# Attention on one core: corrections of the maxima as powers of e on GpSimd, and a quarter of a head's outputs copied by VectorE, three quarters by ScalarE

## The chip, the cores and the metric

The kernel runs on one core of a Trainium2 chip. The metric is the device time of one execution in microseconds (us); of several runs the median counts.

## The reference

One transformer block on `x` of 2 sequences, 2048 tokens, 256 features, all in float32. Six modulation vectors come from a small conditioning input. Then:

```python
h = _layernorm(x) * (1 + ca) + sa
q, k, v = h @ query_proj, h @ key_proj, h @ value_proj     # 16 heads; key size 16, value size 64
attn = softmax(q k^T / 4, axis=1)                          # over the QUERY positions, for each key
o = attn @ v                                               # for each query, a sum over the keys
x = x + ga * (o @ output_proj)
h = _layernorm(x) * (1 + cb) + sb
x = x + gb * down(silu(gate(h)) * up(h))                   # 704 hidden; weights and inputs quantised to FP4 in blocks of 16
```

The softmax runs over the query positions. So a key on a partition has all the 2048 scores that belong to one softmax along its row, and the normalising factor can be multiplied into the value row of that key.

## The kernel before

**Phases.** For each of the 2 sequences (`b`) there is a short preparation (normalised tokens, queries, keys, values) and then attention; at the end one pass over 32 token tiles does the output projection and the feed-forward part. Attention fills most of the time: its first maximum starts at 78.5 us for sequence 0 and at 750.8 us for sequence 1, and its last product starts at 1372.5 us.

**Attention.** Loop variable `j` runs over 256 tiles of 128 keys (16 heads, 16 tiles in each; `i` is the tile within its head). Each tile has two halves of 1024 queries; a half is called a unit here, `u = 2j + half`. For a unit:

- TensorE (`scores`) writes 128 keys by 1024 queries into one of three PSUM slots, `slot[u % 3]`, in 4 matmuls on quarters of the array. It first waits until ScalarE has read the unit three before (`exped`).
- VectorE (`maximum`, line 1070) reduces the slot to the negated maximum `nm` of each key.
- ScalarE (`exponent`, line 812) writes exp(score - maximum) to a ring of 8 tiles in SBUF, `e_sb`, with the row sums in `ssum`.

The two halves of a row have different maxima. For each group of 4 tiles (`g`) the two are reconciled: GpSimd computes the differences `dlt` (lines 1305 to 1309) after tile 4g+3's maxima; ScalarE computes `cor = exp(dlt)` (line 840) in tile 4g+4, after that tile's first exponent; GpSimd then computes the total, its reciprocal as a power of -1 (line 1282), the factors, and the scaled values `vp` for both halves (line 1296).

**Sum over keys.** TensorE (`attend`, line 603) multiplies `vp` by `e_sb` seven tiles later (`jv = j - LAG`, `LAG = 7`) and accumulates a whole head in `acc`, two PSUM banks, 1024 columns. TensorE's order in one `j` is: scores of half 0, half of tile jv's products (8 matmuls), scores of half 1, the other half. On a head's first tile (`begins`) both scores come first and then all 16 matmuls of the tile.

**End of a head.** After the last products of a head, in j with i = 6, VectorE copies `acc[:, 0:512]` to SBUF (`ost`, line 1083), after both of its maxima of that j; ScalarE copies `acc[:, 512:1024]` (line 834) between its two exponents of that j. `took_low` and `took_high` count these. The first products of the next head overwrite `acc` and wait for both counts. GpSimd later splits `ost` in two parts (`split_head`, in tiles with i = 9, 10, 13, 14) and SyncE's queue stores them.

**Order.** Each engine runs the list that the code writes, in that order, with counting semaphores between engines; there is no planner. SyncE only issues DMAs. At the end of sequence 0 GpSimd also computes `rstd` of the next sequence's tokens (`inverse_root`) behind the last `vp`, and TensorE's turning of those tokens (`turn_tokens`, line 457) stands within the last tiles' products.

Of the kernel before, what the change touches and what calls it, by code (L numbers as in the profile page):

```python
# [9 lines left out]
ALU = mybir.AluOpType  # L10
ACT = mybir.ActivationFunctionType
AX = mybir.AxisListType

B, N, D, H, VD, F = 2, 2048, 256, 16, 64, 704
HV = H * VD
P = 128
# [6 lines left out]
SQUARE = (2.0 ** 23 / 12.0) ** 0.5  # L23
FLOOR = 5461.0 * 1024.0
LEAST = 1e-30
GROUP = 4
NG = NT // GROUP
JT = H * NT
JG = JT // GROUP
UNITS = 2 * JT  # L30
# [55 lines left out]
def adaln_block(nc, x, cT, wmod, wq, wk, wv, wo, wgu, wd, out):  # L86
    ctx = ExitStack()
    with ctx:
        def sb(name, shape, dt=F32):
            return ctx.enter_context(nc.sbuf_tensor(name, shape, dt))  # L90
# [4 lines left out]
        def tally(name, step=1):  # L95
            return Tally(ctx.enter_context(nc.semaphore(name)), step)
# [4 lines left out]
        pe, act, dve, pool, sp = nc.tensor, nc.scalar, nc.vector, nc.gpsimd, nc.sync  # L101
# [31 lines left out]
        ost = place("ost", [P, 1024], OST_AT)  # L133
# [3 lines left out]
        ssum = sb("ssum", [P, 4, GROUP, 2])  # L137
        dlt = sb("dlt", [P, 4, GROUP, 2])
# [2 lines left out]
        tot = sb("tot", [P, 4, GROUP])  # L141
        rtot = sb("rtot", [P, 4, GROUP])
        mone = sb("mone", [P, GROUP])
        fac = sb("fac", [P, 4, GROUP, 2])
        st6 = sb("st6", [P, NG, GROUP, 6])
        mv = sb("mv", [P, NG, GROUP, 2])
# [112 lines left out]
        out_out = [tally(f"out_out{s}", 16) for s in range(3)]  # L259

        made_ident, made_half, rstd_made, wv_low = tally("made_ident"), tally("made_half"), tally("rstd_made"), tally("wv_low")
        diff_made, vp_made = tally("diff_made"), tally("vp_made")
        wsq_made, root_made = tally("wsq_made"), tally("root_made")
        wo_split, wd_folded, spread = tally("wo_split"), tally("wd_folded"), tally("spread")
        head_split = tally("head_split")
# [2 lines left out]

        c_exp, wqk_high, wv_high, tok_out = tally("c_exp"), tally("wqk_high"), tally("wv_high"), tally("tok_out")
        part_high, v_act, gu_turned = tally("part_high"), tally("v_act"), tally("gu_turned")  # L270
        dn_turned, exped, cor_made, took_high = tally("dn_turned"), tally("exped"), tally("cor_made"), tally("took_high")
        wgu_high, wdb_high, xq_high, hq_high = tally("wgu_high"), tally("wdb_high"), tally("xq_high"), tally("hq_high")
        silu_made, mix_squared, zx_made = tally("silu_made"), tally("mix_squared"), tally("zx_made")

# [186 lines left out]
        def take_quarter(b, kind, n):  # L461

            q, before = uses[b][kind, n]
            if before:
                pe.wait_ge(*quarter_read(before))
            elif b == 0 and q < 2:
                pe.wait_ge(*mod_cols.past(0))
            elif b and q < 2:
                pe.wait_ge(*exped.past(b * UNITS - 1))
            elif b:  # L470
                pe.wait_ge(*(took_low if q == 2 else took_high).past(b * H - 1))
            return quarter[q]

        def bounds():
# [136 lines left out]
        def project(i):  # L611
            u, r = divmod(i, 2)
            b = i // NT
            if r == 0:
                pe.wait_ge(*o_in[u % 2].past(u // 2))
            if i % NT == 0:
                pe.wait_ge(*wo_split.past(8 * b + 7))
            if i < 3:
                pe.wait_ge(*exped.past(B * UNITS - 1))
            elif i == 3:  # L620
                pe.wait_ge(*took_low.past(B * H - 1))
            else:
                pe.wait_ge(*x2_made.past(i - 1))
            products(proj[i], [(o_r[:, u % 2, 1, c, r * P:(r + 1) * P], o_r[:, u % 2, 0, c, r * P:(r + 1) * P],
                                wo_lo[b][:, c, :], wo_hi[b][:, c, :]) for c in range(8)]).then_inc(proj_mm.sem)
# [189 lines left out]
        def attend_act(b):  # L815
            act.wait_ge(*v_mm.past(2 * (b * NT + EARLY) - 1))
            for p in range(2):
                for r in range(4):
                    act.wait_ge(*part_out[p][r].past(b * NG // 2 + 1))
            for j in range(JT + LAG):  # L820
                jv = j - LAG
                if j == ERING - 2:
                    act.wait_ge(*v_mm.past(2 * (b * NT + 3 * GROUP) - 1))
                if j == ERING - 1:
                    act.wait_ge(*v_mm.past(2 * (b * NT + NT) - 1))
                if b + 1 < B and j in (JT + 4, JT + 6):
                    take_tokens(b + 1, (j - JT) // 2 - 2)
                for half in range(2):
                    if half == 1 and jv >= 0 and jv % NT == NT - 1:
                        h = jv // NT  # L830
                        act.wait_ge(*attended.past(b * JT + jv))
                        if b * H + h >= 1:
                            act.wait_ge(*o_out.past(b * H + h - 1))
                        act.copy(ost[:, 512:1024], acc[:, 512:1024]).then_inc(took_high.sem)
                    if j < JT:
                        exponent(b, j, half)
                    if half == 0 and j % GROUP == 0 and GROUP <= j <= JT:
                        g = j // GROUP - 1
                        act.wait_ge(*diff_made.past(b * JG + g))
                        act.activation(cor[:, g % 4], dlt[:, g % 4], ACT.Exp).then_inc(cor_made.sem)  # L840
                if j < NT - EARLY:
                    take_values_act(b, EARLY + j)
                if j == JT + 2 and b == B - 1:
                    act.wait_ge(*vp_made.past(B * JG - 1))
                    for k in range(2):
                        high(wgu_hi[k][:, :], wguT[:, k, :]).then_inc(wgu_high.sem)
                    stretch(0)
                    square(1)
                    stretch(1)
# [222 lines left out]
        def attend_dve(b):  # L1072
            for j in range(JT + LAG):
                jv = j - LAG
                for half in range(2):
                    if j < JT:
                        maximum(b, j, half)
                if jv >= 0 and jv % NT == NT - 1:
                    h = jv // NT
                    dve.wait_ge(*attended.past(b * JT + jv))  # L1080
                    if b * H + h >= 1:
                        dve.wait_ge(*o_out.past(b * H + h - 1))
                    dve.tensor_copy(ost[:, 0:512], acc[:, 0:512]).then_inc(took_low.sem)  # L1083
                if j < NT - EARLY:
                    take_values_dve(b, EARLY + j)
                if j == JT + 2 and b + 1 < B:
                    stats(b + 1, 0)
                    stats(b + 1, 1)
                    normalise(b + 1, 0)
                    normalise(b + 1, 1)  # L1090
                    stats(b + 1, 2)
                    low_tokens(b + 1, 0)
                    stats(b + 1, 3)
                    normalise(b + 1, 2)
                if j == JT + 6 and b + 1 < B:
                    low_tokens(b + 1, 1)
                    normalise(b + 1, 3)
                if j == JT + 2 and b == B - 1:
                    dve.wait_ge(*wgu_high.past(1))
                    dve.wait_ge(*attended.past(B * JT - 5))  # L1100
                    dve.wait_ge(*got_rows.past(0))
                    for i in range(2):
                        token_moments(i)
                        low(dve, wgu_lo[:, i, :], wguT[:, i, :], wgu_hi[i][:, :]).then_inc(wgu_low.sem)
                    mix_normalise(1)
                    mix_snap(1)
# [162 lines left out]
        def attend_pool(b):  # L1269
            for j in range(JT + LAG):  # L1270
                g = j // GROUP - 1
                s = g % 4
                if j % GROUP == 0 and GROUP <= j <= JT:
                    pool.wait_ge(*cor_made.past(b * JG + g))
                    sem, n = pool_own.next()
                    pool.tensor_tensor(wsum[:, s], cor[:, s], ssum[:, s], ALU.mult).then_inc(sem)  # L1276
# [23 lines left out]
                if j % GROUP == GROUP - 1 and j < JT:  # L1300
                    g, s = j // GROUP, j // GROUP % 4
                    pool.wait_ge(*maxed.past(b * UNITS + 2 * j + 1))
                    if g >= 4:
                        pool.wait_ge(*cor_made.past(b * JG + g - 4))
                    pool.tensor_tensor(dlt[:, s, :, 0], nm[:, s, :, 1], nm[:, s, :, 0], ALU.subtract)  # L1305
                    sem, n = pool_own.next()
                    pool.tensor_tensor(dlt[:, s, :, 1], nm[:, s, :, 0], nm[:, s, :, 1], ALU.subtract).then_inc(sem)
                    pool.wait_ge(sem, n)
                    pool.tensor_scalar(dlt[:, s], dlt[:, s], 0.0, None, ALU.min).then_inc(diff_made.sem)
                if j == JT + 2 and b + 1 < B:  # L1310
                    for g in range(NG):
                        inverse_root(b + 1, g)
# [55 lines left out]
        def gpsimd_program():  # L1368
# [3 lines left out]
                               pattern=[[-1, P]], channel_multiplier=1).then_inc(made_ident.sem)  # L1372
            pool.memset(quarter4[:, :, :], -0.25)
            pool.memset(mone[:, :], -1.0)
            pool.memset(epsilon, EPS)
            pool.memset(zero, 0.0)
            pool.memset(wdT[:, FCH - 1, :], 0.0)
# [56 lines left out]
```

## Time and profile before

| | |
|---|---|
| median of 3 runs | 1696.1 us (1695.29 to 1697.58) |
| profiled execution, its own time | 1700.96 us |
| its span, first to last instruction | 1699.6 us |
| granted TensorE clock, mean | 0.994 of full |
| TensorE matmul busy | 1646.5 us (97%) |
| VectorE busy | 1591.2 us (94%) |
| ScalarE busy | 1364.8 us (80%) |
| GpSimd busy | 779.4 us (46%) |
| moved by DMA | 123.15 MB, mean 72 GB/s |

Busy time is the union of an engine's instructions from first start to last end. Matmuls are pipelined and their ends are modelled, so 97% doesn't mean that TensorE is at its peak. A VectorE or ScalarE instruction's duration includes filling and draining; the next one may start before it ends. "Idle before" is the time in which an engine did nothing before instructions of a group, with the instruction that ended it.

### The profile page before, as it was taken

The numbers are of one execution on the slowest core, as the hardware profiler recorded it, in microseconds if no ns is written. First come the engines' busy times: TensorE is split into PE (matmuls) and PEld (weight loads), VectorE is DVE, ScalarE is ACT, GpSimd is POOL, SyncE is SP. The second block draws the span as 40 slices with busy tenths as digits, with TensorE's granted clock in tenths as the row PEclk, the third lists the DMA queues.
The fourth block names the chain that finished last, engine by engine and source line by source line (L and its number), as shares of the span: only waits on it lengthen the run. The fifth ranks groups of instructions, "written<-read, shape, count | busy, mean of one in ns | idle before, by whom it ended". The sixth has DMA issues, their size and how long they took to land.

```text
span 1699.6 us, 38849 instructions
## 1 busy us (share of the span) xinstructions
PE 1646.5 (97%) x15446; PEld 818.5 (48%) x15446; DVE 1591.2 (94%) x1726; ACT 1364.8 (80%) x2490; POOL 779.4 (46%) x1625
## 2 busy tenths in 40 slices
PE   9999999999999999999999999999999999999998
PEld 8743333333332333664333333333333379999997
DVE  6989999999999999769999999999999869988887
ACT  5389999999999999638999999999999933333332
POOL 3024444544444445303544454566645447644552
PEclk8999999999999999999999999999999999999999
DMA  6202111111111112411111112111111544434420
GB/s 223 72 2 70 51 51 49 45 45 56 61 51 51 47 45 75 156 48 35 46 52 47 45 45 67 53 51 51 46 45 45 154 133 125 149 125 148 153 67 19
DMA packets 83103, 123.15 MB, mean 72 GB/s; under 512 B 4706, under 2 KB 69098, under 8 KB 82922
## 3 DMA queue, kind: packets, MB, share of 16 engines
q1 hardware_dynamic: 82506, 120.15, 22.3%
q8 instruction: 121, 1.98, 0.5%
q14 instruction: 60, 0.49, 0.1%
q10 hardware_dynamic: 416, 0.53, 0.1%
HBM read 74.52 MB, written 46.15 MB: 71 GB/s over the span
## 4 chain that ended last, share of the span: by engine, by line
DVE 65%; PE 29%; ACT 2%; issue 2%; POOL 1%; DMA 1%; SPq 0%; ACTq 0%; POOLq 0%; DVEq 0%
DVE nm L1070 60%; PE acc L436 11%; PE slot L436 9%; PE acc L603 5%; ACT e_sb L812 2%; PE slot L659 1%; DVE ost L1083 1%; PE slot L574 1%; DVE v_sb L1030 1%; DMA v_sb<-in_wmod 0%; PE acc L634 0%; PE slot L457 0%; DVE qs L1137 0%; DMA qk_parts<-e_sb 0%; DVE e_sb L1125 0%
## 5 line engine op out<-in xcount | busy, mean ns | idle before, releaser
L1070 DVE TENSOR_REDUCE nm<-slot 128x1 f32<-128x1024 f32 x1024 | 1166.1, 1213 | 8.1 <-PE slot L574 5.9
L812 ACT ACTIVATE e_sb<-slot,nm 128x1024 f32<-128x1024 f32 x1024 | 1137.3, 1113 | 23.9 <-DVE nm L1070 19.0
L603 PE MATMUL acc<-e_sb,vp 64*64 64x512 f32 x8192 | 1060.7, 594 | 6.7 <-DVE ost L1083 4.7
L574 PE MATMUL slot<-stq,stk 64*64 64x512 f16 x4096 | 412.0, 388 | 21.6 <-ACT e_sb L812 21.6
L574 PEld LDWEIGHTS slot<-stq,stk 64*64 64x64 f16 x4096 | 117.7, 103 | 626.7 <-ACT e_sb L812 589.5
L603 PEld LDWEIGHTS acc<-e_sb,vp 64*64 64x64 f32 x8192 | 283.4, 132 | 188.4 <-issue 74.2
L1305 POOL TENSOR_TENSOR dlt<-nm 128x4 f32<-128x4 f32 x128 | 25.9, 202 | 422.7 <-DVE nm L1070 422.7
L812 ACT ACTIVATION_READ_ACCUMULATOR e_sb<-slot,nm 128x1 f32 x1024 | 199.6, 195 | 0.0
L1296 POOL TENSOR_TENSOR vp<-v_sb,fac 128x512 f32<-128x512 f32 x128 | 133.6, 1044 | 10.2 <-POOL fac L1286 0.3
L1282 POOL TENSOR_TENSOR rtot<-tot,mone 128x4 f32<-128x4 f32 x128 | 132.8, 1038 | 10.0
L1276 POOL TENSOR_TENSOR wsum<-cor,ssum 128x8 f32<-128x8 f32 x128 | 26.0, 203 | 233.4 <-ACT cor L840 233.4
L916 POOL TENSOR_TENSOR ost<-ost,ost_hi 128x256 fp32r<-128x256 f32 x128 | 93.6, 731 | 10.3
L731 ACT CAST xqT_hi<-acc 128x256 fp32r<-128x256 f32 x32 | 11.9, 373 | 106.7 <-PE acc L634 106.6
L436 PE MATMUL slot<-wgu_hi,xqT_hi 128*128 128x352 f32 x256 | 83.6, 327 | 7.1 <-DVE xqT_lo L916 7.1
L885 ACT ACTIVATE e_sb<-slot 128x704 f32<-128x704 f32 x32 | 24.3, 760 | 78.3 <-PE slot L436 78.3
L436 PE MATMUL slot<-wgu_lo,xqT_hi 128*128 128x352 f32 x256 | 82.6, 323 | 0.0
L436 PE MATMUL slot<-wgu_hi,xqT_lo 128*128 128x352 f32 x256 | 82.6, 322 | 0.0
L1362 POOL TENSOR_TENSOR e_sb<-e_sb,qs 128x256 f32<-128x256 f32 x32 | 21.4, 669 | 113.8 <-DVE e_sb L1153 113.8
L1247 POOL CAST ost_hi<-ost 128x256 fp32r<-128x256 f32 x128 | 55.7, 435 | 0.7 <-DVE ost L1083 0.7
L436 PE MATMUL acc<-wdb_hi,hqT_lo 128*128 128x256 f32 x192 | 54.2, 282 | 0.0
L436 PE MATMUL acc<-wdb_hi,upper 128*128 128x256 f32 x192 | 54.0, 281 | 0.0
L436 PE MATMUL acc<-wdb_lo,upper 128*128 128x256 f32 x192 | 54.0, 281 | 0.0
(180 smaller groups left out, 1940.3 us busy)
## 6 DMA issues: line engine op xcount, KB each, us to landing
o_r<-o_heads SPq DMA_DIRECT2D x32, 1024.0 KB, 7.4
stk<-qk_parts SPq DMA_DIRECT2D x128, 128.0 KB
o_heads<-ost_hi SPq DMA_DIRECT2D x64, 256.0 KB, 3.4
o_heads<-ost SPq DMA_DIRECT2D x64, 256.0 KB, 4.1
v_sb<-in_x SPq DMA_DIRECT2D x16, 512.0 KB, 6.6
qk_parts<-e_sb SPq DMA_DIRECT2D x32, 256.0 KB, 2.9
stq<-qk_parts SPq DMA_DIRECT2D x128, 64.0 KB
out<-e_sb SPq DMA_DIRECT2D x32, 128.0 KB, 1.8
```

The source lines that it names most:

```text
L436: mm = pe.matmul(o, a, w, start=(n == 0 and m == 0), stop=(n == len(pairs) - 1 and m == 2))
L574: mm = pe.matmul(slot[s][side * VD:(side + 1) * VD, c * 512:(c + 1) * 512], stk[c * 64:c * 64 + 64, h % 2, i * P + side * VD:i * P + (side ...
L603: mm = pe.matmul(acc[half * VD:(half + 1) * VD, c * 512:(c + 1) * 512], vp[rows, g % 3, gi, half, :], e_v[rows, j % ERING, n0:n0 + 512], s ...
L812: act.activation(e_v[:, j % ERING, half * 1024:(half + 1) * 1024], slot[u % 3][:, :], ACT.Exp, bias=nm[:, g % 4, i, half:half + 1], accum_ ...
L885: act.activation(sg[:, i % 2, :].rearrange("p (a b) -> p a b", b=352), gu[0][:, :].rearrange("p (a b) -> p a b", b=512)[:, :, 0:352], ACT. ...
L916: return eng.tensor_tensor(dst, full, hi.bitcast(F32), ALU.subtract)
L1070: dve.tensor_reduce(nm[:, g % 4, i, half:half + 1], slot[u % 3][:, :], AX.X, ALU.max, negate=True).then_inc(maxed.sem)
L1247: pool.tensor_copy(ost_hi[:, part], ost[:, part]).then_inc(sem)
L1276: pool.tensor_tensor(wsum[:, s], cor[:, s], ssum[:, s], ALU.mult).then_inc(sem)
L1282: pool.tensor_tensor(rtot[:, s, :], tot[:, s, :], mone[:, :], ALU.pow).then_inc(sem)
L1296: pool.tensor_tensor(vp[:, g % 3], v_v[:, i0:i0 + GROUP, h * VD:(h + 1) * VD].unsqueeze(2).to_broadcast([P, GROUP, 2, VD]), fac[:, s].unsq ...
L1305: pool.tensor_tensor(dlt[:, s, :, 0], nm[:, s, :, 1], nm[:, s, :, 0], ALU.subtract)
```

## The change

Three things change.

- The correction `cor` is computed by GpSimd as a power with base e, 8 elements per partition, right after `dlt`. `dlt` is also bounded below at -87.3. ScalarE no longer computes `cor`. GpSimd's sum now waits for `exped` of the first exponent of tile 4g+4 (for the row sums), which before was implied by the wait for ScalarE's `cor`. For a sequence's last group there is no such exponent; there ScalarE copies two sums to a scratch tile after its last exponent and counts `summed`.
- VectorE copies columns 0 to 255 of `acc`, ScalarE columns 512 to 1023 as before and then columns 256 to 511, in a second copy that waits for VectorE's copy (`took_low`). `took_high` is counted by ScalarE's second copy.
- Two waits of TensorE on `took_low` outside the head loop (`take_quarter`, `project`) become waits on `took_high`.

```diff
@@ scalar: attend_act, end of a head and corrections
-                        act.copy(ost[:, 512:1024], acc[:, 512:1024]).then_inc(took_high.sem)
+                        act.copy(ost[:, 512:1024], acc[:, 512:1024])
+                        act.wait_ge(*took_low.past(b * H + h))
+                        act.copy(ost[:, 256:512], acc[:, 256:512]).then_inc(took_high.sem)
                     if j < JT:
                         exponent(b, j, half)
-                    if half == 0 and j % GROUP == 0 and GROUP <= j <= JT:
-                        g = j // GROUP - 1
-                        act.wait_ge(*diff_made.past(b * JG + g))
-                        act.activation(cor[:, g % 4], dlt[:, g % 4], ACT.Exp).then_inc(cor_made.sem)
+                if j == JT:
+                    act.wait_ge(*exped.past((b + 1) * UNITS - 1))
+                    act.copy(sums_last[:, :], ssum[:, (JG - 1) % 4, GROUP - 1, :]).then_inc(summed.sem)
@@ vector: attend_dve
-                    dve.tensor_copy(ost[:, 0:512], acc[:, 0:512]).then_inc(took_low.sem)
+                    dve.tensor_copy(ost[:, 0:256], acc[:, 0:256]).then_inc(took_low.sem)
@@ gpsimd: attend_pool
                 if j % GROUP == 0 and GROUP <= j <= JT:
+                    if j < JT:
+                        pool.wait_ge(*exped.past(b * UNITS + 2 * j))
+                    else:
+                        pool.wait_ge(*summed.past(b))
                     pool.wait_ge(*cor_made.past(b * JG + g))
...
                     pool.wait_ge(*maxed.past(b * UNITS + 2 * j + 1))
-                    if g >= 4:
-                        pool.wait_ge(*cor_made.past(b * JG + g - 4))
...
-                    pool.tensor_scalar(dlt[:, s], dlt[:, s], 0.0, None, ALU.min).then_inc(diff_made.sem)
+                    pool.tensor_scalar(dlt[:, s], dlt[:, s], 0.0, LEAST_EXP, ALU.min, ALU.max).then_inc(diff_made.sem)
+                    pool.wait_ge(*diff_made.past(b * JG + g))
+                    pool.tensor_tensor(cor[:, s], euler[:, :, :], dlt[:, s], ALU.pow).then_inc(cor_made.sem)
@@ tensor: take_quarter and project
-                pe.wait_ge(*(took_low if q == 2 else took_high).past(b * H - 1))
+                pe.wait_ge(*took_high.past(b * H - 1))
...
-                pe.wait_ge(*took_low.past(B * H - 1))
+                pe.wait_ge(*took_high.past(B * H - 1))
```

## Rows read from the trace of the kernel before

**Rows 1.** The page's busy time: engine, us, share, instructions.
```profile
PE 1646.5 (97%) x15446; PEld 818.5 (48%) x15446; DVE 1591.2 (94%) x1726; ACT 1364.8 (80%) x2490; POOL 779.4 (46%) x1625
```

**Rows 2.** Chain of waits, one head of sequence 0: start us, us, what.
```profile
216.67 0.61 DVE ost L1083
...
217.40 1.95 PE acc L603 x16
...
219.60 32.48 DVE nm L1070 x29
...
256.60 1.22 DVE nm L1070
```

**Rows 3.** Timeline at a head's end: start, us, engine, line, operation, count, idle before.
```profile
216.59 0.68 DVE L1083 COPY ost<-acc 128x512 f32<-128x512 f32 x1
216.68 0.58 ACT L834 COPY ost<-acc 128x512 f32<-128x512 f32 x1
...
217.15 1.13 ACT L812 ACTIVATE e_sb<-slot,nm 128x1024 f32<-128x1024 f32 x1
...
217.40 1.95 PE L603 MATMUL acc<-e_sb,vp 64*64 64x512 f32 x16 [0.16 <-DVE ost L1083]
...
219.14 0.42 PE L574 MATMUL slot<-stq,stk 64*64 64x512 f16 x4
...
219.60 3.52 DVE L1070 TENSOR_REDUCE nm<-slot 128x1 f32<-128x1024 f32 x3
```

**Rows 4.** Groups by shape, VectorE and ScalarE: busy us, mean ns, idle.
```profile
L1070 DVE TENSOR_REDUCE nm<-slot 128x1 f32<-128x1024 f32 x1024 | 1166.1, 1213 | 8.1 <-PE slot L574 5.9
...
L1083 DVE COPY ost<-acc 128x512 f32<-128x512 f32 x32 | 21.7, 678 | 0.0
...
L834 ACT COPY ost<-acc 128x512 f32<-128x512 f32 x32 | 18.5, 577 | 0.3 <-PE acc L603 0.3
...
L1170 DVE TENSOR_TENSOR e_sb<-e_sb,acc 128x256 f32<-128x256 f32 x32 | 13.1, 409 | 2.1 <-PE acc L436 2.1
...
L731 ACT CAST xqT_hi<-acc 128x256 fp32r<-128x256 f32 x32 | 11.9, 373 | 106.7 <-PE acc L634 106.6
```

**Rows 5.** Groups by shape: the powers that GpSimd computes.
```profile
L1282 POOL TENSOR_TENSOR rtot<-tot,mone 128x4 f32<-128x4 f32 x128 | 132.8, 1038 | 10.0
...
L1342 POOL TENSOR_TENSOR rstd<-ve,mhalf 128x1 f32<-128x1 f32 x32 | 18.2, 569 | 0.0
```

**Rows 6.** Timeline of one group of four key tiles in mid-head.
```profile
199.62 17.05 DVE L1070 TENSOR_REDUCE nm<-slot 128x1 f32<-128x1024 f32 x15
...
201.36 0.24 POOL L1309 TENSOR_SCALAR dlt<-dlt 128x8 f32<-128x8 f32 x1
...
202.00 1.11 ACT L812 ACTIVATE e_sb<-slot,nm 128x1024 f32<-128x1024 f32 x1
...
203.39 0.20 POOL L1276 TENSOR_TENSOR wsum<-cor,ssum 128x8 f32<-128x8 f32 x1 [1.79 <-ACT cor L840]
...
203.67 0.20 POOL L1279 TENSOR_TENSOR tot<-wsum 128x4 f32<-128x4 f32 x1
...
205.34 1.04 POOL L1296 TENSOR_TENSOR vp<-v_sb,fac 128x512 f32<-128x512 f32 x1
...
206.65 0.41 PE L574 MATMUL slot<-stq,stk 64*64 64x512 f16 x4
...
206.89 1.03 PE L603 MATMUL acc<-e_sb,vp 64*64 64x512 f32 x8
```

**Rows 7.** Timeline at the end of sequence 0.
```profile
682.30 0.24 POOL L1309 TENSOR_SCALAR dlt<-dlt 128x8 f32<-128x8 f32 x1
...
683.20 0.20 POOL L1276 TENSOR_TENSOR wsum<-cor,ssum 128x8 f32<-128x8 f32 x1 [0.65 <-ACT cor L840]
...
688.63 1.09 PE L457 MATMUL slot<-ident,e_sb 128*128 128x128 f32 x8 [0.17 <-DVE e_sb L939]
```

**Rows 8.** Chain of waits after sequence 0's last head.
```profile
697.17 0.49 ACT ost L834
```

More of the change, by code:

```diff
@@ L25 @@
 LEAST = 1e-30
+EULER = 2.718281828459045
+LEAST_EXP = -87.33654
 GROUP = 4
@@ L143, in adaln_block @@
         mone = sb("mone", [P, GROUP])
+        euler = sb("euler", [P, GROUP, 2])
+        sums_last = sb("sums_last", [P, 2])
         fac = sb("fac", [P, 4, GROUP, 2])
@@ L261, in adaln_block @@
         made_ident, made_half, rstd_made, wv_low = tally("made_ident"), tally("made_half"), tally("rstd_made"), tally("wv_low")
-        diff_made, vp_made = tally("diff_made"), tally("vp_made")
+        diff_made, vp_made, cor_made = tally("diff_made"), tally("vp_made"), tally("cor_made")
         wsq_made, root_made = tally("wsq_made"), tally("root_made")
@@ L270, in adaln_block @@
         part_high, v_act, gu_turned = tally("part_high"), tally("v_act"), tally("gu_turned")
-        dn_turned, exped, cor_made, took_high = tally("dn_turned"), tally("exped"), tally("cor_made"), tally("took_high")
+        dn_turned, exped, summed, took_high = tally("dn_turned"), tally("exped"), tally("summed"), tally("took_high")
         wgu_high, wdb_high, xq_high, hq_high = tally("wgu_high"), tally("wdb_high"), tally("xq_high"), tally("hq_high")
@@ L1374, in gpsimd_program @@
             pool.memset(mone[:, :], -1.0)
+            pool.memset(euler[:, :, :], EULER)
             pool.memset(epsilon, EPS)
```

## The prediction

> **What bounds the kernel now.** I read the page's busy times first, then the chain of waits, then the timeline at the place where the chain changes engines. TensorE, VectorE and ScalarE are all close to full [rows 1], so the busy shares alone don't say who sets the pace. The chain does: in each head VectorE's maxima stand for 32.48 us, and the next head starts 256.60 - 219.60 = 37.00 us later [rows 2]. The reader is to see what lies in the other 4.5 us: one more maximum, VectorE's copy of the outputs, TensorE's 16 products, one set of scores, and back to the maxima.
>
> In mid-head VectorE alone is the bound: 15 maxima in 17.05 us [rows 6] with 1.21 us for one [rows 4] are (17.05 - 1.21) / 14 = 1.131 us from start to start. 32 of them are 36.19 us. The copy takes 0.68 us and the maxima overlap by 0.08, so it costs 0.60: 36.79 us. The period is 37.00. The missing 0.2 us is idle time of VectorE, and the timeline shows where [rows 3]: the copy starts at 216.59, so the third maximum after it could start at 216.59 + 0.60 + 2 x 1.13 = 219.45, but starts at 219.60. Its scores started only at 219.14, behind the 16 products that started at 217.40. And those waited for the copies, which ended at 216.59 + 0.68 = 217.27 (VectorE) and 216.68 + 0.58 = 217.26 (ScalarE). So at a head's end VectorE is already ahead of TensorE. What starts the next head is the later of two copies, which today end together.
>
> **The change, part by part.**
>
> *VectorE's copy, 512 to 256 columns.* From 678 ns for 512 columns and 1213 for 1024 the slope is 1.04 ns per column, so 256 columns take 678 - 267 = 411 ns; VectorE's 256-column operation out of the same tensor takes 409 [rows 4]. VectorE's own work per head falls by 0.27 us. The copy would end at 217.00.
>
> *ScalarE's second copy.* It can issue 217.15 - 216.68 = 0.47 us after the first, the distance at which the next instruction now starts [rows 3]. VectorE's copy is over by then (217.00), so the added wait costs nothing. Its duration: the nearest row is ScalarE's 256-column cast out of the same tensor, 373 ns; by the slope from this copy to the 1024-column exponent (1114 - 577 over 512 columns) it would be 308 [rows 3, 4]. I take 373. It ends at 217.15 + 0.37 = 217.52, where the later copy now ends at 217.27: the release of TensorE is 0.25 us later. Lower end: 308 ns, 0.18 us later. Upper end: the second copy waits until the first is drained (0.58 + 0.37), 0.36 us later. A gain is excluded: the second copy can't start before the first is issued, and its end would have to lie before 217.27.
>
> *Who waits.* Queued behind the second copy on ScalarE is the second exponent of that tile: it starts 0.26 us later (the second copy's distance, 0.47 less 0.21 for 256 columns) and ends near 218.54 instead of 218.28; the scores behind the 16 products need it at 219.14 and later, so that is covered. TensorE is not covered: in order, it has nothing to do before the 16 products. They and the following scores move by 0.25. VectorE, now ready at 216.59 + 0.33 + 2.26 = 219.18, waits until 219.60 + 0.25 = 219.85. Its idle time there grows from 0.15 to 0.67 us. VectorE's shorter copy isn't returned, since VectorE was ahead at this point already; the head's period becomes 37.25 us. TensorE's later pace doesn't repair it: what comes after are 29 maxima at VectorE's own pace.
>
> This happens at 15 ends of heads in each sequence: 30 x 0.25 = 7.5 us.
>
> A rule against the split: the Trainium skill (ScalarE: Activation LUTs, What ACT_TABLE_LOAD costs) gives 186 ns plus 0.833 ns per column for an instruction with immediate operands, with about 93 ns of overlap, and Advanced Engine Details and Errata (The Read-Write Bubble) advises large tiles for that reason. By this estimate the copies of 512 and 256 end 0.61 - 0.09 + 0.40 = 0.92 us after the start, 217.60, and 30 ends of heads would cost 9.9 us instead of 7.5. The trace has the 512-column copy at 577 ns, under the page's 613, so I keep the rows.
>
> *Corrections on GpSimd.* ScalarE loses 128 exponents of 8 columns. A gain would need VectorE to wait for what ScalarE releases, and in mid-head it starts a maximum every 1.131 us, right behind the one before [rows 6]: 0. GpSimd gains 128 powers of 8 elements. Rows: 1038 ns for 4 elements, 569 for 1 [rows 5], so 156 ns per element and 1038 + 4 x 156 = 1.66 us. Ends: 1.04 (no dependence on size), 2.08 (twice the row of 4). In mid-head `dlt` is ready at 201.36 + 0.24 = 201.60 and the sum starts at 203.39 [rows 6]. With 0.08 us between dependent steps (203.39 + 0.20 to 203.67) the power is done at 201.60 + 0.08 + 1.66 = 203.34, and the sum starts at 203.42; the exponent that it must also wait for ends at 203.11. So `vp` moves by 0.03 us. It ends now at 206.38, and TensorE takes it at 206.89: some 0.4 us to spare. With 2.08 us `vp` comes 0.45 later: at the edge. Behind it stands a second reserve: TensorE's scores end at 207.06, and VectorE's next start after that is 199.62 + 7 x 1.131 = 207.54. So a power costs nothing until about 1.63 + 0.4 + 0.45 = 2.5 us. The same cover holds for the two-operation `dlt`. In four heads of sequence 1 GpSimd also folds the output weights and its queue is fullest; I count on the same reserve there: 0, or some tenths of a microsecond in all. Its splitting of `ost` starts two tiles after the copies and isn't reached by 0.25 us.
>
> *End of sequence 0.* Here no later exponent stands in between: the sum starts at 683.20, 0.66 us after `dlt` at 682.54. With the power it starts at 682.54 + 0.08 + 1.66 + 0.08 = 684.36, 1.15 us later, and `vp` and the next tokens' `rstd` with it. TensorE has already waited for them, 0.17 us at 688.63 [rows 7], so all 1.15 goes through. ScalarE's last copy is on the chain there as well, at 697.17, and GpSimd's splitting waits for it [rows 8]: 0.25 more. Together 1.4 us. (Ends: 0.54 + 0.18 = 0.7 and 1.57 + 0.36 = 1.9.) At the end of sequence 1 TensorE has the first projections between; I take 0.
>
> **Sum.** 7.5 + 1.4 = 8.9 us, from 0.18 x 30 + 0.7 = 6.1 to 0.36 x 30 + 1.9 = 12.7. The profiled execution's own time is 1700.96 us, so it would be 1709.9. The median shown is 1696.1, 0.3% lower; on it the forecast is 1705.0 (+0.5%).
>
> **Rivals.**
>
> *VectorE's saving counts.* The chain names VectorE's copy at every head's end and its maxima for the rest [rows 2]; a bound engine that sheds 0.27 us should give it back: 30 x 0.27 = 8 us, 1688.0. This needs TensorE to start the products no later than now, and to make up time in the first units of a head. Against it: ScalarE's half already ends with VectorE's (217.26 and 217.27), it can't finish 256 more columns in no time, and VectorE idles right after [rows 3]. Faster.
>
> *Nothing moves.* The 0.13 us between the copies' end and the first product is TensorE's own time and swallows part of the delay, the second copy is shorter than its lower end, and the end of sequence 0 has more slack than the 0.17 us wait says: within 3.4 us, 1696 to 1699.
>
> *GpSimd's chain binds.* If the power of 8 elements with varying exponents takes over 2.5 us, `vp` is late in every group that isn't at the start of a head: with 3.0 us about 0.5 us in some 100 groups, 50 us, near 1755. For it: rows show only the fixed exponents -1 and -0.5. Against it: those two, and 1 and 4 elements, lie on a plausible line that ends far below 2.5.
>
> **How the numbers follow.** The forecast has 0.72, VectorE's saving 0.09, nothing 0.12, GpSimd 0.07. What a measurement of this kernel can tell from no change is about 0.2%, 3.4 us. So faster 0.09, same 0.12, slower 0.79. The forecast's own range is 1702 to 1709. Eight in ten: from 1696, which takes in the upper part of no change, to 1711, which takes in the sum's upper end and a little of GpSimd's case.
>
> **What would show it.** Right: the chain at a head's end goes over ScalarE's copy, not VectorE's; two copies on ScalarE of about 577 and 373 ns, the 16 products starting some 0.9 to 1.0 us after the first (now 0.72); a period of 37.25 us; VectorE's idle time after the copy near 0.7 us; the power at 1.66 us; TensorE's wait at the turn of the sequences near 1.3 us. Wrong: a period at or below 37.00; `vp` on the chain in mid-head; a second copy that starts before 0.47 us or waits for VectorE; a total outside 1702 to 1709.

## The result, and the profile after

The changed kernel took 1703.73 us (median of 5 runs, 1703.44 to 1705.22), the kernel before beside it 1697.58 us (5 runs, 1695.29 to 1698.56): ratio 1.0039, 95% interval 1.0028 to 1.0051, or +6.6 us by the ratio (the medians themselves lie 6.2 us apart). A second comparison of the same two kernels (below, after_again) gave 1.0052, 1.0040 to 1.0065, or +8.8 us by the ratio (medians 10.2 us apart). It is slower, as forecast, by about the size forecast (1705.0 us, range 1696 to 1711).

The profiled execution of the changed kernel took 1703.73 us itself, with a span of 1702.4 us and a mean granted clock of 1.000. The one of before took 1700.96 us at 0.994. Here only 2.8 us lie between them, and a large part of what follows is about that.

The page's busy time after the change (columns as in [rows 1]):

```profile
PE 1639.4 (96%) x15446; PEld 812.3 (48%) x15446; DVE 1582.1 (93%) x1726; ACT 1368.7 (80%) x2396; POOL 977.6 (57%) x1754
```

VectorE sheds 9.1 us against [rows 1], GpSimd gains 198 us, ScalarE 4, although it runs 94 instructions fewer: the small exponents had stood almost wholly within the records of their neighbours (0.2 us of the busy time was theirs alone), while the second copies have 5.2 us to themselves. So the slower kernel has less work on the engine that was its bound in mid-head. The busy shares can't say why.

The chain of waits over one head of sequence 0 (start us, us, what), against [rows 2]:

```profile
213.91 0.39 ACT ost L841
...
214.44 1.95 PE acc L608 x16
...
216.65 1.24 DVE nm L1077
...
251.18 0.39 ACT ost L841
...
253.92 1.24 DVE nm L1077
```

Two things are to be seen. In front of TensorE's 16 products stands ScalarE's second copy, where VectorE's copy stood. And the period, the time from one head to the next, is 253.92 - 216.65 = 37.27 us where it was 37.00 [rows 2]. Between the ends of heads the chain now follows ScalarE's exponents instead of VectorE's maxima; the two run in step there.

The timeline at a head's end (columns as in [rows 3]):

```profile
213.36 0.41 DVE L1090 COPY ost<-acc 128x256 f32<-128x256 f32 x1
213.45 0.57 ACT L839 COPY ost<-acc 128x512 f32<-128x512 f32 x1
...
213.91 0.38 ACT L841 COPY ost<-acc 128x256 f32<-128x256 f32 x1
...
214.44 1.95 PE L608 MATMUL acc<-e_sb,vp 64*64 64x512 f32 x16 [0.43 <-ACT ost L841]
...
216.65 5.79 DVE L1077 TENSOR_REDUCE nm<-slot 128x1 f32<-128x1024 f32 x5 [0.61 <-PE slot L579]
```

VectorE is done at 213.77, ScalarE's second copy at 214.29. The products start 0.99 us after ScalarE's first copy, where it was 217.40 - 216.68 = 0.72 [rows 3]. All of the 0.27 reaches the maxima: the wait of VectorE for the scores is now a row of its own, 0.61 us. Over all heads the same is seen in the waits (engine and line, for whom, total us, times, longest); the line of before, then that of after:

```profile
PE acc L603 <- DVE ost L1083: 4.7, 30, 0.2
```

```profile
PE acc L608 <- ACT ost L841: 12.9, 30, 0.4
```

30 waits grew by 8.2 us in all. The groups by shape (busy us, mean ns, idle) give the prices that [rows 4, 5] had to bound:

```profile
L1321 POOL TENSOR_TENSOR cor<-euler,dlt 128x8 f32<-128x8 f32 x128 | 210.8, 1647 | 10.6
...
L1319 POOL TENSOR_SCALAR dlt<-dlt 128x8 f32<-128x8 f32 x128 | 24.7, 193 | 11.2
...
L839 ACT COPY ost<-acc 128x512 f32<-128x512 f32 x32 | 18.4, 576 | 0.3 <-PE acc L608 0.3
...
L1090 DVE COPY ost<-acc 128x256 f32<-128x256 f32 x32 | 13.1, 410 | 0.0
...
L841 ACT COPY ost<-acc 128x256 f32<-128x256 f32 x32 | 12.3, 383 | 0.0
```

At the end of sequence 0 (timeline; against [rows 7]) the power stands alone between `dlt` and the sum:

```profile
682.63 0.19 POOL L1319 TENSOR_SCALAR dlt<-dlt 128x8 f32<-128x8 f32 x1
...
682.91 1.65 POOL L1321 TENSOR_TENSOR cor<-euler,dlt 128x8 f32<-128x8 f32 x1
...
684.70 0.20 POOL L1288 TENSOR_TENSOR wsum<-cor,ssum 128x8 f32<-128x8 f32 x1
...
687.72 1.95 PE L608 MATMUL acc<-e_sb,vp 64*64 64x512 f32 x16 [0.64 <-POOL vp L1308]
...
690.10 1.09 PE L462 MATMUL slot<-ident,e_sb 128*128 128x128 f32 x8 [0.44 <-DVE e_sb L946]
```

The sum starts 2.07 us after `dlt`, where it was 683.20 - 682.30 = 0.90 [rows 7]. TensorE waits 0.64 + 0.44 = 1.08 us instead of 0.17. From the start of the sequence's last maximum to TensorE's turning (L462; L457 before) it is 9.20 us, and was 8.06: 1.14 us more. This distance is called "the turn" below.

**The account of the two profiled executions.** 30 x 0.273 us (the period is 37.269 in both sequences, 36.996 before) is 8.2 us; the end of sequence 0 brings 1.14: 9.3 us. Seen were 2.8. Both traces can be cut at the starts of the same instructions (the 17th maximum of a sequence, because its first few differ in time where the clock fell just ahead of them):

| stretch | before, us | after, us | difference |
|---|---|---|---|
| up to the first maximum | 78.49 | 74.81 | -3.68 |
| to the 17th maximum | 30.16 | 30.07 | -0.09 |
| to the last maximum of sequence 0 | 571.91 | 576.02 | +4.11 |
| to ScalarE's last copy of the values (L767; L772 after) | 63.58 | 64.58 | +1.00 |
| to the 17th maximum of sequence 1 | 37.29 | 35.86 | -1.43 |
| to the last maximum of sequence 1 | 571.91 | 576.00 | +4.09 |
| to the end | 346.29 | 345.07 | -1.22 |

The third and the sixth row are the heads, 15 x 0.273 = 4.10 each, as it should be. The fourth is the 1.14 of the turn, but for 0.14. The other rows became shorter. The stretches at three of these places, of before and then of after (from:to, length, busy time of each engine, granted clock, DMA share, GB/s):

```profile
0.00:20.00 20.00, 17.55 (x89) 17.12 (x90) 10.68 (x42) 6.46 (x10) 4.18 (x15) 0.70 0.83 288
745.00:755.00 10.00, 7.42 (x43) 4.63 (x41) 5.03 (x6) 4.58 (x11) 0.00 (x0) 0.83 0.14 51
1390.00:1400.00 10.00, 7.81 (x49) 7.29 (x48) 8.07 (x11) 3.25 (x5) 6.10 (x8) 0.83 0.01 2
```

```profile
0.00:20.00 20.00, 17.62 (x112) 16.58 (x113) 12.56 (x51) 8.18 (x13) 4.21 (x16) 1.00 0.83 290
745.00:755.00 10.00, 7.41 (x48) 4.87 (x47) 6.48 (x8) 4.66 (x12) 0.00 (x0) 1.00 0.14 50
1390.00:1400.00 10.00, 6.41 (x43) 5.68 (x42) 9.72 (x14) 2.71 (x5) 5.13 (x7) 1.00 0.27 85
```

The number before the last two is the granted clock, the share of TensorE's full speed. The profiled execution of before ran parts of all three places at TensorE's lower level (1.2 GHz), that of after none. By the table the changed kernel gained 3.68 + 0.09 us at the first place, 1.43 at the second and 1.22 at the third, 6.4 in all: 9.3 - 6.4 - 0.1 = 2.8, as was seen. So the next question was whether the change has anything to do with the clock.

### The profile page after: what moved, and what is told of

Read it like the earlier page. It is cut to its first block, busy times and chain, and to the rows that moved or that the text cites. A ratio compares the mean times of both kernels' runs of the same rounds, so it can differ in the third digit from the quotient of the medians.

```text
span 1702.4 us, 38892 instructions
## 1 busy us (share of the span) xinstructions
PE 1639.4 (96%) x15446; PEld 812.3 (48%) x15446; DVE 1582.1 (93%) x1726; ACT 1368.7 (80%) x2396; POOL 977.6 (57%) x1754
## 4 chain that ended last, share of the span: by engine, by line
ACT 41%; PE 28%; issue 22%; DVE 8%; POOL 1%; DMA 0%; SPq 0%; POOLq 0%; ACTq 0%; DVEq 0%
ACT e_sb L817 39%; PE acc L441 10%; PE slot L441 9%; PE acc L608 5%; DVE nm L1077 4%; PE slot L664 1%; ACT ost L841 1%; PE slot L579 1%; DVE v_sb L1037 1%; ACT ost L839 0%; PE acc L447 0%; PE acc L639 0%; DVE qs L1144 0%; DMA qk_parts<-e_sb 0%; PE slot L462 0%
## 5 line engine op out<-in xcount | busy, mean ns | idle before, releaser
L1321 POOL TENSOR_TENSOR cor<-euler,dlt 128x8 f32<-128x8 f32 x128 | 210.8, 1647 | 10.6
L1308 POOL TENSOR_TENSOR vp<-v_sb,fac 128x512 f32<-128x512 f32 x128 | 133.4, 1042 | 10.2 <-POOL fac L1298 0.3
L1294 POOL TENSOR_TENSOR rtot<-tot,mone 128x4 f32<-128x4 f32 x128 | 129.2, 1009 | 10.0
```

The lines of the kernel that those rows point to most:

```text
L1294: pool.tensor_tensor(rtot[:, s, :], tot[:, s, :], mone[:, :], ALU.pow).then_inc(sem)
L1308: pool.tensor_tensor(vp[:, g % 3], v_v[:, i0:i0 + GROUP, h * VD:(h + 1) * VD].unsqueeze(2).to_broadcast([P, GROUP, 2, VD]), fac[:, s].unsq ...
L1321: pool.tensor_tensor(cor[:, s], euler[:, :, :], dlt[:, s], ALU.pow).then_inc(cor_made.sem)
```

## Experiments

The theory: TensorE's release at each head's end is set by the later of two copies; the change makes ScalarE's later by 0.27 us; the power costs something only at the end of sequence 0; the clock of the three places varies from run to run in either kernel. The rivals: the powers cost time in mid-head too; VectorE's shorter copy gives something back; the change itself raised the clock. Each kernel was timed beside the kernel before.

**before_again: the kernel before, unchanged.**

> The kernel before, unchanged, for a second trace. In the first trace TensorE's granted clock was 0.70 of full from 0 to 20 us and lower again near 749 and 1395 us; the changed kernel's trace has 1.00 throughout. If these drops belong to an execution, this trace may lack them, and then its own time is near 1694.5 us (1700.96 less some 6.5 us that the three places cost), with the head's period at 37.00 us. If they belong to the kernel's program, they are there again at the same three places. Times: within 0.2% of the kernel before.

1697.58 us (11 runs), ratio 1.0004 (0.9995 to 1.0013); its profiled execution took 1698.29 us at a mean clock of 0.997. The same three stretches:

```profile
0.00:20.00 20.00, 17.65 (x109) 16.44 (x110) 11.74 (x46) 7.32 (x12) 4.17 (x15) 0.91 0.83 292
745.00:755.00 10.00, 9.62 (x51) 6.70 (x52) 5.64 (x6) 5.71 (x13) 0.00 (x0) 0.83 0.14 50
1390.00:1400.00 10.00, 8.80 (x54) 8.56 (x55) 7.98 (x12) 3.37 (x5) 4.28 (x8) 0.83 0.01 2
```

Neither alternative of the expectation came out whole: the places recur, but the amount differs (0.91 at the start, where it was 0.70), and the first maximum starts at 75.66 us instead of 78.49, which is what the profiled execution was faster by. The places aren't fixed for every variant: in less_vector (below) the last stretch at the lower level begins at 1525 us instead of near 1395, and power_twice has four, near 776, 1209, 1462 and 1595 us, and none in the first 20.

**split_only: the copies alone, added to the kernel before, with the two waits outside the head loop; the corrections stay on ScalarE.**

```
-  act.copy(ost[:, 512:1024], acc[:, 512:1024]).then_inc(took_high.sem)
+  act.copy(ost[:, 512:1024], acc[:, 512:1024])
+  act.wait_ge(*took_low.past(b * H + h))
+  act.copy(ost[:, 256:512], acc[:, 256:512]).then_inc(took_high.sem)
-  dve.tensor_copy(ost[:, 0:512], acc[:, 0:512]).then_inc(took_low.sem)
+  dve.tensor_copy(ost[:, 0:256], acc[:, 0:256]).then_inc(took_low.sem)
```

> Only the copies changed (VectorE 256 columns, ScalarE 512 and 256), the corrections stay on ScalarE. Release theory (the head's period is set by the later copy): period 37.27 us as in the changed kernel, 30 x 0.27 = 8.1 us over the kernel before, and TensorE's wait at the turn of the sequences unchanged at 0.17 us. VectorE theory (its saving counts): period 36.73, 8 us less.

1706.29 us (5 runs), ratio 1.0053 (1.0039 to 1.0067), period 37.269 us, the turn 8.06 us as before. Its timeline at a head's end:

```profile
215.57 0.57 ACT L834 COPY ost<-acc 128x512 f32<-128x512 f32 x1
...
216.04 0.38 ACT L836 COPY ost<-acc 128x256 f32<-128x256 f32 x1
...
216.56 1.95 PE L603 MATMUL acc<-e_sb,vp 64*64 64x512 f32 x16 [0.43 <-ACT ost L836]
```

The same 0.99 us, the same wait of 0.43. The whole cost per head is the copies'. Three of its runs had a mean clock of 0.996 (1706.1 to 1706.7 us), like 15 runs of the kernel before (median 1698.3): 8.0 us, where 30 x 0.273 is 8.2.

**powers_only: the changed kernel with the copies as before** (and the two waits outside the head loop).

```
-  dve.tensor_copy(ost[:, 0:256], acc[:, 0:256]).then_inc(took_low.sem)
+  dve.tensor_copy(ost[:, 0:512], acc[:, 0:512]).then_inc(took_low.sem)
-  act.copy(ost[:, 512:1024], acc[:, 512:1024])
-  act.wait_ge(*took_low.past(b * H + h))
-  act.copy(ost[:, 256:512], acc[:, 256:512]).then_inc(took_high.sem)
+  act.copy(ost[:, 512:1024], acc[:, 512:1024]).then_inc(took_high.sem)
```

> Only the corrections moved to GpSimd, the copies as before (512 and 512). Release theory: period 37.00 us, nothing in mid-head; the sum after the last group of sequence 0 comes 1.15 us later, so about +1.1 us in all, within what can be told from no change. A rival in which ScalarE's freed 25 us count: faster by up to 0.1 us per group, 12 us. A rival in which GpSimd's longer chain delays the scaled values in every group: slower by 0.1 us or more per group, 12 us or more.

1697.12 us (11 runs), ratio 1.0004 (0.9995 to 1.0013); period 36.996 us, the turn 9.20. 128 powers of 1.65 us cost nothing in mid-head, and 1.14 us at the turn. The interval of the medians holds that 1.14 us (ratio 1.0007) and 0. Runs at the same clock show it: at 0.999 they took 1696.9 and 1697.1 us and those of the kernel before 1695.9 (median of 17), at 0.998 1698.4 and 1697.3 (median of 19), at 1.000 1695.6 to 1696.2 and 1694.4 (one run); only at 0.997 there is no difference (1697.6 and 1698.2 against 1698.3).

**last_on_scalar: the changed kernel, but the last group of each sequence has its correction from ScalarE's exponent.**

```
-  act.wait_ge(*exped.past((b + 1) * UNITS - 1))
-  act.copy(sums_last[:, :], ssum[:, (JG - 1) % 4, GROUP - 1, :]).then_inc(summed.sem)
+  act.wait_ge(*diff_made.past(b * JG + JG - 1))
+  act.activation(cor[:, (JG - 1) % 4], dlt[:, (JG - 1) % 4], ACT.Exp).then_inc(summed.sem)
...
-  pool.wait_ge(*cor_made.past(b * JG + g))
+  if j < JT:
+      pool.wait_ge(*cor_made.past(b * (JG - 1) + g))
...
+  if g < JG - 1:
...
       pool.tensor_tensor(cor[:, s], euler[:, :, :], dlt[:, s], ALU.pow).then_inc(cor_made.sem)
```

> The changed kernel, but each sequence's last group has its correction computed by ScalarE again. If the power behind the last group is the second term of the sum, TensorE's wait for the next sequence's tokens falls from some 1.3 us to near 0.2 us and the last products of sequence 0 end 1.1 us earlier; the period stays 37.27. Total: 1.1 us under the changed kernel, +8 us against the kernel before. If this term is given back later (in the preparation of sequence 1), the total doesn't move.

1704.72 us (5 runs), ratio 1.0048 (1.0033 to 1.0062); period 37.269 us, the turn 8.04. The timeline there:

```profile
684.42 0.19 POOL L1320 TENSOR_SCALAR dlt<-dlt 128x8 f32<-128x8 f32 x1
...
685.03 0.20 ACT L847 ACTIVATE cor<-dlt 128x8 f32<-128x8 f32 x1
685.32 0.20 POOL L1289 TENSOR_TENSOR wsum<-cor,ssum 128x8 f32<-128x8 f32 x1 [0.71 <-ACT cor L847]
```

The sum is back at 0.90 us after `dlt`, and the 1.16 us of the turn are gone. The median doesn't show it: the one run at a mean clock of 1.000 took 1702.0, and those of the changed kernel at this clock 1703.4 to 1704.0; but its one run at 0.996 took 1708.0, and the changed kernel's at this clock 1707.8 and 1708.0. These are few runs. The trace shows the turn; that the total falls with it isn't shown by this kernel.

**less_vector, less_both, less_scalar: the kernel before with one or both copies at half width from the second head on.** The columns that are then copied by nobody are left out of the output.

```
less_vector, less_both:
-  dve.tensor_copy(ost[:, 0:512], acc[:, 0:512]).then_inc(took_low.sem)
+  n = 256 if h else 512
+  dve.tensor_copy(ost[:, 0:n], acc[:, 0:n]).then_inc(took_low.sem)
less_scalar, less_both:
-  act.copy(ost[:, 512:1024], acc[:, 512:1024]).then_inc(took_high.sem)
+  n = 768 if h else 1024
+  act.copy(ost[:, 512:n], acc[:, 512:n]).then_inc(took_high.sem)
```

> The kernel before, but from the second head of each sequence on VectorE copies only columns 0 to 255 and nobody copies 256 to 511 (this part of the output is left out). ScalarE's copy stays at 512 columns. Release theory: ScalarE's copy still ends 0.58 us after its start, as late as VectorE's did, so the period stays 37.00 us and VectorE idles 0.27 us more per head: no change in time. VectorE theory: period 36.73, 28 x 0.27 = 7.6 us less.

> As less_vector, and ScalarE copies only columns 512 to 767 (columns 256 to 511 and 768 to 1023 are left out from the second head on). Release theory: the later copy now ends near 217.06 instead of 217.27 on the first trace's times, so the products and the scores behind them come 0.21 us earlier, while VectorE is ready at 219.18: scores for it at 219.39, period 36.79 us, 28 x 0.21 = 5.9 us less. VectorE theory: no further change against less_vector, 36.73. If both copies were free of price: period 37.00.

> The kernel before, but from the second head of each sequence on ScalarE copies only columns 512 to 767 (768 to 1023 are left out); VectorE copies its 512 as before. Release theory, the later copy decides: VectorE's ends as before, so the period stays 37.00 us and the time doesn't change. Rival, only ScalarE's copy counts: period 36.79, 6 us less.

less_vector: 1698.24 us (11 runs), ratio 1.0004 (0.9995 to 1.0013), period 36.996. less_scalar: 1697.74 (11), 1.0002 (0.9994 to 1.0011), period 36.968. less_both: 1691.44 (5), 0.9963 (0.9950 to 0.9975), -6.3 us by the ratio (medians 6.0 apart), period 36.783. A head's end in the timelines of less_vector, less_scalar and less_both:

```profile
214.94 0.41 DVE L1084 COPY ost<-acc 128x256 f32<-128x256 f32 x1
215.02 0.57 ACT L834 COPY ost<-acc 128x512 f32<-128x512 f32 x1
...
215.74 1.95 PE L603 MATMUL acc<-e_sb,vp 64*64 64x512 f32 x16 [0.16 <-ACT ost L834]
...
217.95 4.66 DVE L1070 TENSOR_REDUCE nm<-slot 128x1 f32<-128x1024 f32 x4 [0.34 <-PE slot L574]
```

```profile
216.89 0.68 DVE L1084 COPY ost<-acc 128x512 f32<-128x512 f32 x1
216.98 0.36 ACT L835 COPY ost<-acc 128x256 f32<-128x256 f32 x1
...
217.67 1.95 PE L603 MATMUL acc<-e_sb,vp 64*64 64x512 f32 x16
```

```profile
214.94 0.41 DVE L1085 COPY ost<-acc 128x256 f32<-128x256 f32 x1
215.02 0.36 ACT L835 COPY ost<-acc 128x256 f32<-128x256 f32 x1
...
215.53 1.95 PE L603 MATMUL acc<-e_sb,vp 64*64 64x512 f32 x16
```

The products start 0.72, 0.69 and 0.51 us after ScalarE's copy. Halving either copy alone moves them by 0.00 and 0.03; halving both by 0.21, and that comes out of the period in full: 28 x 0.213 is 6.0 us (the copies of each sequence's first head stay whole). In less_vector the 0.27 us that VectorE sheds turn up as 0.34 us of waiting for the scores. That settles the rival of VectorE's saving: it returns nothing, not because VectorE has no part in the bound, but because at this place it is ahead already.

**all_scalar: ScalarE copies all 1024 columns in one instruction, VectorE none (VectorE's copy and the waits on it go).**

```
-  act.copy(ost[:, 512:1024], acc[:, 512:1024]).then_inc(took_high.sem)
+  act.copy(ost[:, :], acc[:, :]).then_inc(took_high.sem)
```

> The kernel before, but ScalarE copies all 1024 columns of a head in one instruction and VectorE none. Release theory: the copy takes 577 + 512 x 0.75 to 1.05 = 0.96 to 1.11 us and ends 0.37 to 0.52 us later than now: period 37.37 to 37.52, 11 to 16 us over the kernel before, although VectorE has 0.60 us less work in each head. VectorE theory: 36.40, 18 us less.

1710.17 us (5 runs), ratio 1.0078 (1.0065 to 1.0090), +13.2 us by the ratio (medians 12.8 apart); period 37.422, and 30 x 0.426 is 12.8. Its timeline:

```profile
215.38 1.00 ACT L833 COPY ost<-acc 128x1024 f32<-128x1024 f32 x1
...
216.52 1.95 PE L602 MATMUL acc<-e_sb,vp 64*64 64x512 f32 x16 [0.58 <-ACT ost L833]
```

The products start 1.14 us after the copy's start, 0.42 later than before, and the period is 0.43 longer. VectorE has 0.60 us less to do in each head, and the kernel is 13 us slower: the further one goes in the direction of the change, the more it costs.

**power_twice and power_and_one: the changed kernel, in which GpSimd computes a further power into an unused tensor before each correction.** In the first it is one of 8 elements, in the second one of a single element.

```
power_twice:
+  pool.tensor_tensor(spare[:, :, :], euler[:, :, :], dlt[:, s], ALU.pow)
power_and_one:
+  pool.tensor_tensor(spare[:, 0, 0:1], euler[:, 0, 0:1], dlt[:, s, 0, 0:1], ALU.pow)
```

> The changed kernel with the power of 8 elements computed twice (the second result is used), so that some 3.4 us stand between the differences and the sum instead of 1.7. By the two reserves of the prediction about 2.5 us are free: the rest, 0.9 us, is paid in each group outside a head's start, 3 groups in a head, 90 in all: 80 us over the changed kernel, period near 39.9. If GpSimd's chain has more reserve than that, less; if the scaled values are off the critical path altogether, no change.

> The changed kernel with one more power of a single element per partition ahead of each correction: some 0.57 us more, 2.2 us in all between the differences and the sum. With two powers of 8 (3.27 us) two groups in a head paid 0.73 us each, so 2.54 us are free: here nothing is paid in mid-head and the period stays 37.27. Only the end of sequence 0 and the four heads with folding can cost, 0.6 us and some tenths: about +1 us over the changed kernel. If the cost were proportional to GpSimd's time instead: a third of power_twice's, 20 us or more.

power_twice: 1769.02 us (4 runs), ratio 1.0418 (1.0404 to 1.0432), 65 us above the changed kernel where 80 were expected. Its chain in mid-head:

```profile
231.83 1.65 POOL spare L1322
233.48 1.62 POOL cor L1323
...
237.15 1.05 POOL vp L1309
238.25 1.09 PE acc L609 x8
...
239.59 1.24 DVE nm L1078
```

Here GpSimd is the bound: `vp` releases TensorE, TensorE the next maximum. The period in sequence 0 is 38.74 us, 1.47 more; that is two groups of a head paying 0.73 each, not three. Against the changed kernel the intervals between maxima are longer in tile 3 of a head (0.72 us) and in tile 15 (0.73); nothing is paid in tile 7, where TensorE starts the next head's products behind the copies, and nothing in tile 11. Why tile 11 pays nothing isn't shown. The two powers take 1.65 + 1.62 = 3.27 us, so 3.27 - 0.73 = 2.5 us are free. The heads of sequence 1 in which GpSimd also folds the output weights took up to 42.3 us: there the queue has less reserve.

power_and_one: 1707.89 us (5 runs), ratio 1.0058 (1.0044 to 1.0071). Its groups by shape:

```profile
L1323 POOL TENSOR_TENSOR cor<-euler,dlt 128x8 f32<-128x8 f32 x128 | 211.0, 1648 | 0.0
L1322 POOL TENSOR_TENSOR spare<-euler,dlt 128x1 f32<-128x1 f32 x128 | 71.2, 557 | 10.7
```

1648 + 557 = 2.2 us in front of each sum, and the period is 37.271, as in the changed kernel: still free. From the 17th to the last maximum of sequence 1 it took 577.05 us, 1.05 more than in the changed kernel; this lies in the four heads with the folding, a quarter of a microsecond in each. At a mean clock of 0.999 its runs took 1706.3 and 1707.0, those of the changed kernel 1705.2 and 1705.3.

**after_again: the changed kernel, unchanged.**

> The changed kernel, unchanged, for its share of stretches at half of TensorE's clock. Its five runs so far had a granted clock of 0.999 to 1.000, those of the kernel before 0.995 to 1.000. Clock theory (the whole costs 9.4 us, and runs at a higher clock hid a part of it): wherever a run shows 1.000 it takes near 1703.6 us, and a run at 0.996 near 1707; if the mean clock is now that of the kernel before, the difference of the medians is near 9. Rival (the change gives back 3 us somewhere): the difference stays near 6.5 us at equal clocks.

1707.79 us (5 runs, 1703.98 to 1708.02), ratio 1.0052 (1.0040 to 1.0065), period 37.269. Three of its five runs had a mean clock of 0.996 to 0.997, so the change doesn't keep the clock up everywhere. With the clock of each run beside its time (medians, from all comparisons that show the clock of each run):

| mean granted clock | before, us | changed, us | difference |
|---|---|---|---|
| 1.000 | 1694.4 (1 run) | 1703.7 (5) | 9.4 |
| 0.999 | 1695.9 (17) | 1705.3 (2) | 9.4 |
| 0.997 | 1698.3 (6) | 1707.8 (1) | 9.5 |
| 0.996 | 1698.3 (15) | 1707.9 (2) | 9.7 |

At the same mean clock the change costs 9.4 to 9.7 us, and the account from the traces says 9.3. The comparisons (6.6 and 8.8 us by the ratio) are lower and apart from one another; all 10 runs of the changed kernel against all 62 of the kernel before give 1704.6 against 1697.4, or 7.2 us.

That is not only the luck of few runs: at one of the three places the change seems to move the clock itself, and this rival stays open. In all eight profiled executions in which ScalarE computes a sequence's last correction (before, before_again, split_only, last_on_scalar, less_vector, less_scalar, less_both, all_scalar) the clock falls to its lower level 67 to 68 us after sequence 0's last maximum. In four of the five in which GpSimd computes it (after, after_again, powers_only, power_and_one) it doesn't; power_twice falls at 71 us. From ScalarE's last copy of the values to the 17th maximum of sequence 1 it took 37.17 to 37.51 us where the clock fell and 35.86 to 35.91 where it didn't, so the lower stretch costs 1.3 to 1.7 us. In the runs, 9 of 30 with the power behind the last group had a mean clock of 1.000, and 2 of 104 without it. So the 1.14 us of the turn, paid at equal clocks, come with a gain of about the same size from the clock, and little of them is left in the medians. No experiment moved the turn without the power, so a cause isn't shown. At the first place powers_only and power_and_one have the same lower stretch as split_only, less_vector and less_both (clock 0.74), but only after, after_again and power_twice have none; whether the change matters there can't be told from these.

No kernel that does all the work came out faster than the one before. With halves of 512 the two copies end within 0.01 us of one another [rows 3], so by the slopes no other split of the columns should end earlier, and the corrections on GpSimd return nothing. An order in which TensorE has something else to do at a head's end wasn't tried.

## Why the prediction was right

- **The bound at a head's end.** Held. The later of two copies starts the next head; VectorE is ahead there. Shown from both sides: less_vector and less_scalar change nothing, less_both gives 6.3 us, split_only and all_scalar cost what their later copy costs.
- **The term of 0.25 us for each head.** Right mechanism, slightly small: 0.273. The second copy took 383 ns, not 373, and was issued 0.46 us after the first; the first product came 0.14 to 0.15 us after the copies' end, where 0.13 was read from [rows 3]. So 8.2 us instead of 7.5.
- **The wait for VectorE's copy costs nothing.** Held: VectorE ended at 213.77, the second copy was issued at 213.91.
- **The price of the copies.** The trace put the second copy at 383 ns and the first at 576. The Trainium skill (ScalarE: Activation LUTs, What ACT_TABLE_LOAD costs) has 186 ns plus 0.833 ns per column for an ACTIVATE with immediate scale and bias; an estimate from it for copies of these widths is 399 and 613. The profile lists these instructions as COPY. all_scalar's 1003 ns for 1024 columns gives a slope of (1003 - 576) / 512 = 0.834 ns, as the page has it; the fixed part here is some 150 ns (576 - 512 x 0.834), below the 186. The estimate by this page of the skill was 0.33 us at a head's end; these runs show 0.27.
- **VectorE's saving isn't returned.** Held; its idle time in front of the maxima is 0.61 us in the row (forecast 0.67 from 0.15).
- **The power of 8 elements.** 1.66 us forecast, 1.647 measured; the line through 1 and 4 elements holds, also with varying exponents. Its 2.5 us of cover in mid-head is confirmed by power_twice. The expectation for that kernel let three groups of a head pay; two do.
- **The end of sequence 0.** 1.15 us forecast, 1.14 measured at TensorE's turning, with it in powers_only and without it in last_on_scalar. TensorE's waits there are 1.08 us, not 1.3: 0.2 of the 1.14 don't show as a wait, and where they lie isn't shown. That "all 1.15 goes through" holds at equal clocks; by the traces the clock gives back 1.3 to 1.7 us at the same place, and the prediction had no such term. Its further 0.25 us for the last copy behind it isn't shown: with the new copies and the old corrections ScalarE's last copy of the values starts 63.45 and 63.32 us after the last maximum (split_only, last_on_scalar), with the old copies 63.22 to 63.84.
- **The sum.** 8.9 us forecast, 9.3 by the account, 9.4 to 9.7 at equal clocks. That the first comparison gave 6.6, and the profiled execution 1703.73 us instead of the 1709.9 forecast for it, was no part of the reasoning: the sum was put on an execution that lost some 6 us to the lower clock, and the clock of its stretches wasn't looked at. The forecast was scaled to the median, and that the measured median lies only 1.3 us from it is in part luck: it holds a sum 0.4 us too small, a median of the kernel before that was 1.5 us higher this time, and four runs of five at a mean clock of 1.000.

## What to carry to other kernels

Where several engines empty an accumulator that an in-order engine waits for, only the end of the last copy counts: split so that all end together, and read from the timeline who is already idle there before taking work off the engine that is the bound elsewhere. A chain of waits names one of two copies that end 0.01 us apart, and it says nothing of what the other would do. Before comparing two profiled executions to a few tenths of a per cent, compare the granted clock stretch by stretch, and don't take it as given that a change leaves the clock alone.

## What the runs showed of the hardware

- TensorE's clock fell to its lower level at the same three places in both traces of the kernel before (the first 20 us, near 750 and near 1395 us), and nowhere in the profiled execution of the changed kernel (mean clock 1.000). In the first 20 us of before, 8 transpositions of 128x128 (L457) took 421 ns on average; the median of all 64 of that line is 273. In the stretch 745 to 755 us TensorE was busy for 7.42 of 10 us with the drop and 7.41 without, so these records don't tell why it comes. The 62 runs of the kernel before with a clock beside them range from 1694.4 us (mean clock 1.000) to 1700.1 (0.995): about 1 us for each thousandth.
- GpSimd's power costs by the element in each partition: 557 ns for 1, 1009 for 4, 1647 for 8. Just before it, the limit at two ends in one instruction (L1319) took 193 ns, where the limit at one end took 0.24 us [rows 6].
- ScalarE's copy of 256 columns took 383 ns as the second of two and 363 alone (less_both, the copies at half width).
